# Token scatter by quarters with one semaphore each, first expert tiles from pair one, last batch regrouped in six and four tiles

## The chip, the cores and the metric

The program runs on one core of one Trainium2 chip. The metric is device time in microseconds. Five engines work side by side and meet through semaphores: TensorE (PE, with PEld for its weight loads), VectorE (DVE), ScalarE (ACT), GpSimd (POOL) and SyncE (SP), which issues most DMAs.

## The reference

The input is 8 batches of 512 tokens with 128 features. Each token is normalised; then two branches are added to the input:

```
xn = layernorm(x)
x  = x + mamba(xn) + moe(xn)
mamba: project to 2*256 channels, causal convolution and silu in both directions,
       dA = exp(delta*A), dBx = delta*B*u, h[l] = dA[l]*h[l-1] + dBx[l]  (16 states per channel),
       y = sum over states of h*C + D*u, times silu(z), both directions added, projected to 128
moe:   16 experts, 4 chosen per token by score; softmax gates over the four;
       expert e: w2[e] @ gelu(w1[e] @ xn + b1[e]) + b2[e]; gated sum of the four
```

## The kernel before, in words

The program has three stages.

**Preparation.** For each of the 8 batches PE, ACT and DVE compute the scan's inputs and store them in DRAM. DVE does for each batch a convolution (L1382, then twelve chained L1387), L1404, and pairs of L1409, L1415, L1422 and L1428. In the same time POOL scatters the tokens to their experts: each token's row (128 features, an id, a gate) goes to four slots of `slots_d`. There are four rounds k, one for each chosen expert. A round copies the gates of all 32 token tiles into the rows `xn` (L758, one copy of 128x32), waits for the copy, and issues 32 indirect DMAs (L762), one for each tile of 128 tokens. As the next round overwrites the gates in the rows, it first waits until all 32 DMAs of the last round have landed. All of them count on the semaphore `scattered`. SP waits for the whole count in `read_first` before it reads the first two expert tiles.

**Scan.** Eight batches follow, each in 32 steps called pairs. A pair q has two states (j = 0, 1) of 128 channels: ACT makes the decays (L1001), PE puts the B rows in PSUM (L1231, L1234), DVE multiplies where needed (L1478) and scans (two L1490), POOL multiplies the states by C (L794), PE adds them up (L1170). In some pairs DVE does the product instead (L1498): pairs 1, 4 and 7 of the first batch (`FIRST_VECTOR`) and the last ten pairs of the last batch (`LAST_VECTOR`). A state lives in a ring of 8, so DVE can be at most 8 pairs ahead of the sums.

Beside the pairs, PE and ACT compute the 80 expert tiles of 256 slots, ten in each batch. A written order (`EVENTS`, `FIRST`, `LAST`) says at which pair PE does each event: T turns the rows of a tile (L1184), U0 and U1 are the two halves of the first layer (L1191), D is the second layer (L1199), G and O are the Mamba output projection of the batch before, X and Y prepare the next batch. PE is in order: an event at pair q stands behind the B rows of pair q and ahead of those of pair q+1. ACT empties the event's PSUM bank two to four pairs later, and runs gelu for a group of tiles in one go (L969). After a D, ACT scales the rows (L947) and POOL adds them with an indirect DMA into one of two accumulators in DRAM (L779), by even and odd tile. In the first batch T comes at pairs 5, 7, 9, 11, 13, then as in the others.

**Tail.** SP reads the stored Mamba outputs (`mixed_d`) and both accumulators (L704). DVE adds them (L1537, L1543, L1545, L1548), and SP stores the result.

Of the kernel before, what the change touches and what calls it, by code (L numbers as in the profile page):

```python
# [14 lines left out]
D = 128  # L15
BATCH, L = 8, 512
TOK = BATCH * L
NT = TOK // P
TPB = L // P
DIN = 256  # L20
NH = DIN // P
# [5 lines left out]
E, TOPK = 16, 4  # L27
FF = 512
FC = FF // P
# [4 lines left out]
MPB = NTILE // BATCH  # L34
# [24 lines left out]

FIRST_VECTOR = (1, 4, 7)  # L60
VECTOR = ()
# [79 lines left out]

FIRST_T = [5, 7, 9, 11, 13] + T_STEP[GROUP:]
FIRST_U = [q + 2 for q in FIRST_T]
# [3 lines left out]
for _j in range(MPB):  # L147
    FIRST[FIRST_T[_j]].append(("T", _j, 1, False))
    if _j >= GROUP:
        FIRST[FIRST_T[_j] + 1].append(("D", _j - GROUP, 0, False))  # L150


LAST_T = [0, 2, 4, 7, 9, 12, 15, 17, 20, 22]
LAST_U = [2, 4, 6, 9, 11, 13, 16, 18, 21, 23]
LAST_D = [(1, 5, True), (3, 6, True), (5, 7, True), (8, 8, True), (10, 9, True), (17, 0, False), (19, 1, False),
          (22, 2, False), (24, 3, False), (25, 4, False), (27, 5, False), (28, 6, False), (29, 7, False), (30, 8, False),
          (31, 9, False)]
LAST = [[] for _ in range(PAIRS)]
# [8 lines left out]
LAST_LAG = 4  # L167
LAST_GELU = [16, 28]
LAST_BURSTS = [[12, 13], [24, 25]]
LAST_STEP = [p + (LAST_LAG - 2 if p < 6 or 15 < p < 19 else LAST_LAG - 1 if p < 9 or 13 < p < 22 or p == 26 else  # L170
# [47 lines left out]
def hidden_slot(b, j):  # L218

    if isinstance(b, int) and b == BATCH - 1 and j >= GROUP:  # L220
        return j if j < GROUP + 2 else j - GROUP - 2
    return j % GROUP
# [15 lines left out]
WTS_DMAS = 7  # L238
XQ = 4
XN_ACT = 3  # L240
DEST_LAG = 1
# [16 lines left out]
def wait(eng, semaphore, value):  # L258

    if not isinstance(value, int) or value > 0:  # L260
        eng.wait_ge(semaphore, value)
# [13 lines left out]
def bank_written(eng, sems, b, what, j, m, before=False):  # L275

    wait(eng, sems[f"m{m}_ready"], uses(b, m, what, j, before) + 1)
# [7 lines left out]
def bank_emptied(eng, sems, b, what, j, m, before=False):  # L285

    wait(eng, sems[f"m{m}_free"], uses(b, m, what, j, before) + 1)


def build_kernel(nc, x_in, consts_in, chan_in, inw_in, xproj_in, dtw_in, outw_in,  # L290
                 route_in, b2_in, w1_in, w2_in, out):
    with ExitStack() as ctx:  # L292
# [3 lines left out]
        def sem(name):  # L296
            return ctx.enter_context(nc.semaphore(name))
# [59 lines left out]
        def carve(n):  # L357
# [13 lines left out]
        state = carve(H_RING * 2 * L).rearrange("p (r j l) -> p r j l", r=H_RING, j=2)  # L371
        late = delta[:, 0].rearrange("p q l -> p (q l)").rearrange("p (t f s) -> p t f s", t=2, f=FC)
        hidden_all = carve(GROUP * FC * S)
        hidden = hidden_all.rearrange("p (t f s) -> p t f s", t=GROUP, f=FC)
        hidden = [hidden[:, t] for t in range(GROUP)] + [late[:, t] for t in range(2)]

        acc = [t[:, 0:BATCH * TPB * D].rearrange("p (b n) -> p b n", b=BATCH)
               for t in (decay.rearrange("p r j l -> p (r j l)"), hidden_all)]
        scanned = [t[:, 0, :, :].rearrange("p q l -> p (q l)").rearrange("p (b n) -> p b n", b=BATCH // 2) for t in (delta, du)]
# [80 lines left out]
            kw_ready bias_ready behind_ready experts_ready xn_act_ready shift_ready score_ps score_ready sel_ready logit_ps keys_ps chosen_ready rank_ps pos_ready gdiff_ready gexp_ready  # L460
            gates_ready tag_ready ids_ready acc_filled scattered v_chain pad_ready drop_ready xz_ps
            xpad_ready z_ps z_sb v_ready u_ready xd_ps xd_sb part1_ready
# [5 lines left out]
            mixed_out mixed_in sp_step pool_step acc_ready acc_last out_done"""  # L468
        s = {n: sem(n) for n in names.split()}
        x_loaded = [sem(f"x_in{i}") for i in range(XQ)]  # L470
        c_in = [sem(f"c_in{i}") for i in range(C_RING)]
# [24 lines left out]
        def _(sp):  # L496
# [78 lines left out]
            def read_first():  # L575

                sp.wait_ge(s["scattered"], 16 * NT * TOPK)
                sp.wait_ge(s["b2_out"], 16)
                sp.wait_ge(s["experts_ready"], 1)
                for j in range(W_RING):  # L580
                    read_up(j, j, j)
                    read_down(j, j)
# [70 lines left out]
            def batch(b, par):  # L653
                last = isinstance(b, int) and b == BATCH - 1
                for q in range(PAIRS + 2):
# [24 lines left out]
                    if 1 <= q <= PAIRS:  # L680
                        reload(b, q - 1)

            for r in range(C_RING):
# [8 lines left out]

            sp.wait_ge(s["mixed_out"], 16 * (BATCH - 1))
            for j in (GROUP, GROUP + 1):
                m = [e[2] for step in LAST for e in step if e[:2] == ("D", j) and not e[3]][0]
                bank_written(sp, s, BATCH - 1, "D", j, m)
            half = BATCH // 2
            for k, n in ((0, half), (1, half - 1)):
                sp.dma_start(scanned[k][:, 0:n, :], mixed_d[k * half:k * half + n].rearrange("b p n -> p b n")).then_inc(s["mixed_in"], 16)
            sp.wait_ge(s["scan_done"], DECAYS * BATCH)  # L700
            for i in range(W_RING):
# [23 lines left out]
        def _(pool):  # L725
# [28 lines left out]
            pool.wait_ge(s["gates_ready"], 1)  # L754
            for k in range(TOPK):

                wait(pool, s["scattered"], 16 * NT * k)
                nc.gpsimd.tensor_copy(xn[:, :, D + 1], gates[:, :, k]).then_inc(s["tag_ready"], 1)  # L758
                pool.wait_ge(s["tag_ready"], k + 1)
                pool.wait_ge(s["pos_ready"], min(k, 1) + 1)  # L760
                for t in range(NT):
                    pool.indirect_dma_start(slots_d, bass.IndirectOffsetOnAxis(  # L762
                        ap=pos[:, t * TOPK + k:t * TOPK + k + 1], axis=0), xn[:, t, :], None).then_inc(s["scattered"], 16)
            pool.wait_ge(s["acc_filled"], 16 * ACC_DMAS)
# [46 lines left out]
        def _(act):  # L811
# [119 lines left out]
            def empty(b, q, par=None):  # L931

                for what, j, m, before in events(b, q):
                    bank = m_ps[m]
                    bank_written(act, s, b, what, j, m, before)
                    if what == "T":
                        last = nc.scalar.copy(rowsT[:, :], bank[:, 0:S])
                    elif what in ("U0", "U1"):
                        for f in range(2):
                            c = 2 * (what == "U1") + f  # L940
                            last = nc.scalar.activation(hidden[hidden_slot(b, j)][:, c, :], bank[:, f * S:(f + 1) * S], ACT.Identity,  # L941
                                                        bias=w1[:, j % W_RING, FF + c:FF + c + 1])
# [17 lines left out]
            def gelus(b, n, now, bursts):  # L960

                for k in range(GROUP):
                    if not isinstance(b, int) or 0 <= b < BATCH:
                        if k == 0:

                            for what, m in (("U0", 1), ("U1", 0)):
                                bank_emptied(act, s, b, what, GROUP * (n + 1) - 1, m)
                        h = hidden[hidden_slot(b, GROUP * n + k)].rearrange("p f s -> p (f s)")
                        nc.scalar.activation(h, h, ACT.Gelu).then_inc(s["gelu_done"], 1)  # L969
                    if k in (1, 3):  # L970
                        empty(now, bursts[k // 2])
# [286 lines left out]
        def _(dve):  # L1258
# [274 lines left out]

            dve.wait_ge(s["mixed_in"], 32)
            for b in range(BATCH - 1):
# [75 lines left out]
```

## Time and profile before

| | us |
|---|---|
| median of 3 runs (1123.13 to 1128.26) | 1124.62 |
| the profiled execution's own time | 1122.8 |
| its span, first to last instruction | 1121.0 |
| DVE busy | 1035.2 (92%) |
| ACT busy | 938.8 (84%) |
| PE busy | 928.8 (83%) |
| POOL busy | 910.8 (81%) |
| mean granted TensorE clock | 0.943 |

The busy shares are means over the three stages. Preparation runs to about 253 us, the scan to about 1097 us, the tail to the end. An engine's row in a timeline gives its start, its duration and, in brackets, how long the engine was idle before it and what ended that idle time.

### The profile page before, as it was taken

What the parts mean: (1) busy time and instruction counts of PE and PEld (TensorE: products, weight loads), DVE (VectorE), ACT (ScalarE), POOL (GpSimd) and SP (SyncE); (2) the same over time, 40 slices, a digit from 0 to 9 for tenths busy, and PEclk for the clock granted to TensorE, in tenths of its full rate; (3) what the DMA queues carried; (4) which work ended last, traced back from release to release, by engine and by line L of the source; (5) the groups of instructions that cost most, each with busy time, mean ns of one, the idle gap of its engine ahead of it and who ended that gap; (6) DMA issues with size and microseconds to landing.
All of it is one profiled execution on the core that took longest, in us unless ns stands there. A gap on an engine that the chain in (4) does not pass through costs nothing. (4 is left out here: it accounts for less than half of the span.)

```text
span 1121.0 us, 21799 instructions
## 1 busy us (share of the span) xinstructions
PE 928.8 (83%) x5866; PEld 737.1 (66%) x5866; DVE 1035.2 (92%) x1356; ACT 938.8 (84%) x1732; POOL 910.8 (81%) x552
## 2 busy tenths in 40 slices
PE   5476887663889999999999989899999999987993
PEld 2233332232778787878887877788788777877872
DVE  8878998859999999999999989999999999986996
ACT  5258888865899999999999989999899999987940
POOL 4277878657579999999999998989999999986771
PEclk9789989775899999999999999999999999998996
DMA  9974565486756877687677767777876877665568
GB/s 304 365 253 185 193 228 191 164 295 208 238 163 175 219 192 208 182 235 194 188 207 208 194 174 212 198 196 180 233 201 162 233 192 206 164 164 142 126 143 250
DMA packets 153027, 228.87 MB, mean 204 GB/s; under 512 B 36220, under 2 KB 97948, under 8 KB 147620
## 3 DMA queue, kind: packets, MB, share of 16 engines
q1 hardware_dynamic: 125764, 208.39, 58.7%
q0 software_dynamic: 27136, 19.02, 11.8%
q8 instruction: 51, 0.84, 0.3%
q14 instruction: 76, 0.62, 0.2%
HBM read 161.84 MB, written 69.64 MB: 207 GB/s over the span
## 5 line engine op out<-in xcount | busy, mean ns | idle before, releaser
L1490 DVE TENSOR_TENSOR_SCAN arena<-arena,ps 128x512 f32<-128x512 f32 x512 | 598.1, 1202 | 0.6
L794 POOL TENSOR_TENSOR arena<-arena 128x1024 f32<-128x1024 f32 x243 | 521.1, 2476 | 49.8 <-DVE arena L1490 49.6
L1001 ACT ACTIVATE arena<-delta,a_neg 128x511 f32<-128x511 f32 x512 | 340.9, 728 | 6.7 <-DVE arena L1437 3.3
L779 POOL DMA_INDIRECT acc_d<-yrows,tags x160 | 253.3, 1583 | 46.5 <-issue 37.1
L1170 PE MATMUL ps<-ident,arena 128*128 128x128 f32 x2048 | 274.6, 278 | 7.5 <-POOL arena L794 5.1
L1478 DVE TENSOR_TENSOR ps<-du,ps 128x512 f32<-128x512 f32 x352 | 232.9, 677 | 27.2 <-PE ps L1234 25.1
L1170 PEld LDWEIGHTS ps<-ident,arena 128*128 128x128 f32 x2048 | 237.1, 144 | 20.6 <-POOL arena L794 5.6
L762 POOL DMA_INDIRECT slots_d<-arena,pos x128 | 152.8, 1193 | 46.3 <-issue 44.7
L1199 PE MATMUL ps<-w,arena 128*128 128x128 f32 x1248 | 173.8, 282 | 3.9 <-ACT arena L969 2.9
L1199 PEld LDWEIGHTS ps<-w,arena 128*128 128x128 f32 x1248 | 153.7, 191 | 14.4 <-issue 4.9
L1191 PE MATMUL ps<-rowsT,w 128*128 128x256 f32 x640 | 153.9, 384 | 10.5 <-ACT arena L952 7.5
L922 ACT ACTIVATE arena<-arena 128x256 f32<-128x256 f32 x320 | 145.5, 511 | 0.0
L1191 PEld LDWEIGHTS ps<-rowsT,w 128*128 128x128 f32 x640 | 118.2, 192 | 29.6 <-ACT arena L952 9.3
L941 ACT ACTIVATE arena<-ps,w 128x256 f32<-128x256 f32 x312 | 123.7, 477 | 4.8 <-PE ps L1191 4.4
L1231 PE MATMUL ps<-ident,arena 128*128 128x128 f32 x640 | 95.4, 279 | 22.0 <-DVE arena L1490 17.7
L1231 PEld LDWEIGHTS ps<-ident,arena 128*128 128x128 f32 x640 | 74.7, 144 | 27.5 <-DVE arena L1490 20.0
L947 ACT ACTIVATE yrows<-ps,tags 128x128 f32<-128x128 f32 x160 | 49.8, 365 | 51.3 <-PE ps L1201 40.8
L969 ACT ACTIVATE arena<-arena 128x1024 f32<-128x1024 f32 x78 | 79.1, 1054 | 0.2
L1234 PE MATMUL ps<-parts,sel 128*128 128x512 bf16 x176 | 60.3, 396 | 12.8 <-DVE arena L1490 12.6
L1387 DVE SCALAR_TENSOR_TENSOR arena<-arena,chan 128x512 f32<-128x512 f32 x96 | 64.2, 741 | 0.0
L1184 PE MATMUL ps<-ident,rows 128*128 128x128 f32 x160 | 34.1, 296 | 33.4 <-ACT arena L941 20.6
L1084 PE MATMUL ps<-arena 128*128 128x256 f32 x64 | 24.0, 541 | 33.5 <-ACT arena L843 33.5
(150 smaller groups left out, 904.6 us busy)
## 6 DMA issues: line engine op xcount, KB each, us to landing
arena<-c_d SPq DMA_DIRECT2D x128, 512.0 KB, 4.3
w<-w_dram SPq DMA_DIRECT2D x80, 258.0 KB
w<-w_dram SPq DMA_DIRECT2D x80, 256.0 KB
rows<-slots_d SPq DMA_DIRECT2D x80, 130.0 KB
slots_d<-delta SPq DMA_DIRECT2D x5, 2015.0 KB, 19.5
delta_d<-arena SPq DMA_DIRECT2D x8, 1024.0 KB, 3.9
du_d<-delta SPq DMA_DIRECT2D x8, 1024.0 KB, 6.4
delta<-delta_d SPq DMA_DIRECT2D x8, 1024.0 KB, 7.1
```

What stands on the lines that cost most here:

```text
L762: pool.indirect_dma_start(slots_d, bass.IndirectOffsetOnAxis(ap=pos[:, t * TOPK + k:t * TOPK + k + 1], axis=0), xn[:, t, :], None).then_in ...
L779: pool.indirect_dma_start(acc_d[j % W_RING], bass.IndirectOffsetOnAxis(ap=tags[:, j, a, 0:1].bitcast(I32), axis=0), yrows[:, j % W_RING, a ...
L794: nc.gpsimd.tensor_tensor(state[:, q % H_RING], state[:, q % H_RING], c_rows[:, r % C_RING], ALU.mult).then_inc(s["prod_done"], 1)
L922: last = nc.scalar.activation(scaled_du[scaled_slot(g, j)][:, t, :], duT[:, par, t, :], ACT.Identity, scale=bT[:, par, t, n:n + 1])
L941: last = nc.scalar.activation(hidden[hidden_slot(b, j)][:, c, :], bank[:, f * S:(f + 1) * S], ACT.Identity, bias=w1[:, j % W_RING, FF + c: ...
L1001: nc.scalar.activation(decay[:, q % DA_RING, j, lo:lo + L - 1], delta[:, par, dh, lo:lo + L - 1], ACT.Exp, scale=a_neg[:, dh, 2 * g + j:2 ...
L1170: last = nc.tensor.matmul(y_ps[:, h, t * P:(t + 1) * P], state[:, q % H_RING, j, t * P:(t + 1) * P], ident[:, :], is_transpose=True, start ...
L1191: last = nc.tensor.matmul(bank[:, f * S:(f + 1) * S], w1[:, slot, c * P:(c + 1) * P], rowsT[:, :], start=True, stop=True)
L1199: nc.tensor.matmul(bank[:, a * P:(a + 1) * P], kept[:, c, a * P:(a + 1) * P], w2[:, slot, c, :], start=c == 0, stop=False)
L1231: last = nc.tensor.transpose(bank[:, t * P:(t + 1) * P], scaled_du[scaled_slot(g, j)][:, t, h * P:(h + 1) * P], ident[:, :])
L1478: nc.vector.tensor_tensor(b_ps[:, ROW[q, j], j, :], du[:, par, q % DH, :], b_row, ALU.mult)\
L1490: nc.vector.tensor_tensor_scan(state[:, q % H_RING, j, way], decay[:, q % DA_RING, j, way], b_ps[:, ROW[q, j], j, way], 0.0, ALU.mult, ALU ...
```

## The change

Three things change together.

1. The scatter. `TQ = 4` quarters of 8 token tiles each have a semaphore `scattered[g]`. A round's gates are copied by quarters, 16 copies of 128x8 in all. The first four copies come ahead of the first DMA. From the second group of 8 DMAs on, the copy for the next round of the quarter issued before this one follows each group, and waits only for that quarter's own DMAs. SP waits for the four semaphores one after the other.
2. The first batch. T comes at pairs 1, 4, 7, 10, 13 instead of 5, 7, 9, 11, 13, and DVE does no product there.
3. The last batch and the tail. The ten tiles are run through gelu in groups of six and four, at ACT steps 17 and 28, instead of five and five at 16 and 28. Some T, U and D move; the last five D come one pair earlier. The bursts emptied within the first gelu group are those of pairs 14 and 15 (G and O) instead of 12 and 13. Two hidden tiles live in `gate` and `skip` instead of `delta`, the first accumulator's landing place is no longer the decays' memory but older input's, and SP reads the stored Mamba outputs in seven DMAs from pair 20 on instead of two near the end. SP starts to read the accumulators once the last B rows are written instead of after the last scan.

```diff
-FIRST_VECTOR = (1, 4, 7)
+FIRST_VECTOR = ()
-FIRST_T = [5, 7, 9, 11, 13] + T_STEP[GROUP:]
+FIRST_T = [1, 4, 7, 10, 13] + T_STEP[GROUP:]
-LAST_T = [0, 2, 4, 7, 9, 12, 15, 17, 20, 22]
-LAST_U = [2, 4, 6, 9, 11, 13, 16, 18, 21, 23]
-LAST_D = [(1, 5, True), (3, 6, True), (5, 7, True), (8, 8, True), (10, 9, True), (17, 0, False), (19, 1, False),
-          (22, 2, False), (24, 3, False), (25, 4, False), (27, 5, False), (28, 6, False), (29, 7, False), (30, 8, False),
-          (31, 9, False)]
+LAST_T = [0, 2, 4, 7, 9, 12, 16, 18, 20, 22]
+LAST_U = [2, 4, 6, 9, 11, 13, 18, 20, 22, 23]
+LAST_D = [(1, 5, True), (3, 6, True), (5, 7, True), (8, 8, True), (10, 9, True), (16, 0, False), (19, 1, False),
+          (21, 2, False), (24, 3, False), (25, 4, False), (26, 5, False), (27, 6, False), (28, 7, False), (29, 8, False),
+          (30, 9, False)]
...
-LAST_GELU = [16, 28]
-LAST_BURSTS = [[12, 13], [24, 25]]
+MIXED_FROM = 20
+LAST_TILES = [range(GROUP + 1), range(GROUP + 1, MPB)]
+LAST_GELU = [17, 28]
+LAST_BURSTS = [[14, 15], [24, 25]]
...
-                sp.wait_ge(s["scattered"], 16 * NT * TOPK)
+                for g in range(TQ):
+                    sp.wait_ge(scattered[g], 16 * (NT // TQ) * TOPK)
+                    sp.sem_inc(s["sp_step"], 1)
...
+                    if last and MIXED_FROM <= q < MIXED_FROM + BATCH - 1:
+                        n = q - MIXED_FROM
+                        sp.dma_start(scanned[2 * n // BATCH][:, n % (BATCH // 2), :], mixed_d[n]).then_inc(s["mixed_in"], 16)
...
-            sp.wait_ge(s["scan_done"], DECAYS * BATCH)
+            sp.wait_ge(s["b_ready"], len(FILLS) * BATCH)
...
-            for k in range(TOPK):
-
-                wait(pool, s["scattered"], 16 * NT * k)
-                nc.gpsimd.tensor_copy(xn[:, :, D + 1], gates[:, :, k]).then_inc(s["tag_ready"], 1)
-                pool.wait_ge(s["tag_ready"], k + 1)
+            part = NT // TQ
+
+            def tag(n):
+
+                k, g = n // TQ, n % TQ
+                own = slice(g * part, (g + 1) * part)
+                wait(pool, scattered[g], 16 * part * k)
+                nc.gpsimd.tensor_copy(xn[:, own, D + 1], gates[:, own, k]).then_inc(s["tag_ready"], 1)
+
+            for n in range(TQ):
+                tag(n)
+            for n in range(TOPK * TQ):
+                k, g = n // TQ, n % TQ
+                pool.wait_ge(s["tag_ready"], n + 1)
                 pool.wait_ge(s["pos_ready"], min(k, 1) + 1)
-                for t in range(NT):
+                for t in range(g * part, (g + 1) * part):
                     pool.indirect_dma_start(slots_d, bass.IndirectOffsetOnAxis(
-                        ap=pos[:, t * TOPK + k:t * TOPK + k + 1], axis=0), xn[:, t, :], None).then_inc(s["scattered"], 16)
+                        ap=pos[:, t * TOPK + k:t * TOPK + k + 1], axis=0), xn[:, t, :], None).then_inc(scattered[g], 16)
+                if n > 0 and n - 1 + TQ < TOPK * TQ:
+                    tag(n - 1 + TQ)
...
-            dve.wait_ge(s["mixed_in"], 32)
+            dve.wait_ge(s["mixed_in"], 16 * (BATCH - 1))
```

## Rows read from the trace of the kernel before

**Rows 1.** The page's first part: busy time and share of each engine.
```profile
PE 928.8 (83%) x5866; PEld 737.1 (66%) x5866; DVE 1035.2 (92%) x1356; ACT 938.8 (84%) x1732; POOL 910.8 (81%) x552
```

**Rows 2.** Timeline of POOL: start, duration, line, operation; in brackets idle before it.
```profile
47.80 0.36 POOL L758 COPY arena<-gates 128x32 f32<-128x32 f32 x1 [21.72 <-DMA slots_d<-delta]
...
93.16 1.70 POOL L762 DMA_INDIRECT slots_d<-arena,pos  x1 [0.30 <-issue]
99.09 7.10 POOL L758 COPY arena<-gates 128x32 f32<-128x32 f32 x1 [4.22 <-DMA slots_d<-arena,pos]
106.46 0.98 POOL L762 DMA_INDIRECT slots_d<-arena,pos  x1 [0.28 <-POOL arena L758]
...
117.32 1.04 POOL L762 DMA_INDIRECT slots_d<-arena,pos  x1 [0.30 <-issue]
...
142.17 1.38 POOL L762 DMA_INDIRECT slots_d<-arena,pos  x1 [0.31 <-issue]
143.86 1.02 POOL L762 DMA_INDIRECT slots_d<-arena,pos  x1 [0.30 <-issue]
...
158.33 0.24 POOL L758 COPY arena<-gates 128x32 f32<-128x32 f32 x1 [1.45 <-DMA slots_d<-arena,pos]
...
207.44 0.96 POOL L762 DMA_INDIRECT slots_d<-arena,pos  x1 [0.30 <-issue]
213.19 3.93 POOL L758 COPY arena<-gates 128x32 f32<-128x32 f32 x1 [4.79 <-DMA slots_d<-arena,pos]
217.40 0.98 POOL L762 DMA_INDIRECT slots_d<-arena,pos  x1 [0.28 <-POOL arena L758]
...
240.46 0.96 POOL L762 DMA_INDIRECT slots_d<-arena,pos  x1 [0.30 <-issue]
248.63 0.97 POOL L762 DMA_INDIRECT slots_d<-arena,pos  x1 [7.22 <-issue]
...
267.99 0.96 POOL L762 DMA_INDIRECT slots_d<-arena,pos  x1 [0.30 <-issue]
```

**Rows 3.** Timeline of DVE in preparation, and at the start of the first batch.
```profile
46.30 1.75 DVE L1353 TENSOR_TENSOR arena<-arena 128x1536 f32<-128x1536 bf16 x1
...
96.92 8.03 DVE L1387 SCALAR_TENSOR_TENSOR arena<-arena,chan 128x512 f32<-128x512 f32 x12
104.87 1.22 DVE L1404 TENSOR_SCALAR du<-arena 128x2048 f32<-128x2048 f32 x1
...
119.06 8.03 DVE L1387 SCALAR_TENSOR_TENSOR arena<-arena,chan 128x512 f32<-128x512 f32 x12
127.02 1.21 DVE L1404 TENSOR_SCALAR du<-arena 128x2048 f32<-128x2048 f32 x1
...
157.10 2.35 DVE L1422 SCALAR_TENSOR_TENSOR arena<-ps,arena 128x1024 f32<-128x1024 f32 x2
...
215.80 1.21 DVE L1404 TENSOR_SCALAR du<-arena 128x2048 f32<-128x2048 f32 x1
...
235.57 1.23 DVE L1404 TENSOR_SCALAR du<-arena 128x2048 f32<-128x2048 f32 x1 [7.23 <-ACT arena L874]
...
258.76 0.67 DVE L1478 TENSOR_TENSOR ps<-du,ps 128x512 f32<-128x512 f32 x1
260.58 1.23 DVE L1498 TENSOR_TENSOR arena<-arena 128x1024 f32<-128x1024 f32 x1 [1.15 <-DMA arena<-c_d]
...
271.38 4.59 DVE L1498 TENSOR_TENSOR arena<-arena 128x1024 f32<-128x1024 f32 x1
...
285.74 1.22 DVE L1498 TENSOR_TENSOR arena<-arena 128x1024 f32<-128x1024 f32 x1
```

**Rows 4.** Timeline of PE: the first T of the first batch.
```profile
275.44 0.69 PE L1184 MATMUL ps<-ident,rows 128*128 128x128 f32 x2 [1.58 <-DMA tags<-slots_d]
```

**Rows 5.** DVE's waits from 990 us on: sum, times, longest.
```profile
DVE ps L1478 <- PE ps L1234: 12.7, 5, 5.0
```

**Rows 6.** The chain of work that ended last, in order of time.
```profile
1098.48 6.76 DMA acc_d<-yrows,tags
...
1115.33 0.69 DVE arena L1548
```

More of the change, by code:

```diff
@@ L239 @@
 XQ = 4
+TQ = 4
 XN_ACT = 3
@@ L371, in build_kernel @@
         state = carve(H_RING * 2 * L).rearrange("p (r j l) -> p r j l", r=H_RING, j=2)
-        late = delta[:, 0].rearrange("p q l -> p (q l)").rearrange("p (t f s) -> p t f s", t=2, f=FC)
+        late = [flat.rearrange("p (f s) -> p f s", f=FC) for flat in (gate[:, 0].rearrange("p h t c -> p (h t c)"),
+                                                                       skip[:, 0].rearrange("p h l -> p (h l)"))]
         hidden_all = carve(GROUP * FC * S)
         hidden = hidden_all.rearrange("p (t f s) -> p t f s", t=GROUP, f=FC)
-        hidden = [hidden[:, t] for t in range(GROUP)] + [late[:, t] for t in range(2)]
+        hidden = [hidden[:, t] for t in range(GROUP)] + late
         acc = [t[:, 0:BATCH * TPB * D].rearrange("p (b n) -> p b n", b=BATCH)
-               for t in (decay.rearrange("p r j l -> p (r j l)"), hidden_all)]
+               for t in (arena[:, TURNED_AT:turned_end], hidden_all)]
         scanned = [t[:, 0, :, :].rearrange("p q l -> p (q l)").rearrange("p (b n) -> p b n", b=BATCH // 2) for t in (delta, du)]
@@ L460, in build_kernel @@
             kw_ready bias_ready behind_ready experts_ready xn_act_ready shift_ready score_ps score_ready sel_ready logit_ps keys_ps chosen_ready rank_ps pos_ready gdiff_ready gexp_ready
-            gates_ready tag_ready ids_ready acc_filled scattered v_chain pad_ready drop_ready xz_ps
+            gates_ready tag_ready ids_ready acc_filled v_chain pad_ready drop_ready xz_ps
             xpad_ready z_ps z_sb v_ready u_ready xd_ps xd_sb part1_ready
@@ L469, in build_kernel @@
         s = {n: sem(n) for n in names.split()}
+        scattered = [sem(f"scattered{i}") for i in range(TQ)]
         x_loaded = [sem(f"x_in{i}") for i in range(XQ)]
@@ L681, in batch @@
                         reload(b, q - 1)
+                    if last and q == MIXED_FROM:
+                        sp.wait_ge(s["mixed_out"], 16 * b)
+                        sp.sem_inc(s["sp_step"], 1)
+                        sp.wait_ge(s["decay_ready"], DECAYS * b)
+                        sp.sem_inc(s["sp_step"], 1)
+                        sp.wait_ge(s["dbx_done"], len(DBX) * b)
+                        sp.sem_inc(s["sp_step"], 1)
+                    if last and MIXED_FROM <= q < MIXED_FROM + BATCH - 1:
+                        n = q - MIXED_FROM
+                        sp.dma_start(scanned[2 * n // BATCH][:, n % (BATCH // 2), :], mixed_d[n]).then_inc(s["mixed_in"], 16)
             for r in range(C_RING):
@@ L691, in _ @@
             batch(BATCH - 1, 1)
[L693 to L699, printed above, removed]
-            sp.wait_ge(s["scan_done"], DECAYS * BATCH)
+            sp.wait_ge(s["b_ready"], len(FILLS) * BATCH)
             for i in range(W_RING):
@@ L938, in empty @@
                     elif what in ("U0", "U1"):
+                        if isinstance(b, int) and b == BATCH - 1 and j == GROUP:
+                            act.wait_ge(s["y_free"], NH * b)
                         for f in range(2):
@@ L960, in gelus @@
             def gelus(b, n, now, bursts):
-                for k in range(GROUP):
+                tiles = LAST_TILES[n] if isinstance(b, int) and b == BATCH - 1 else range(GROUP * n, GROUP * (n + 1))
+                for k, j in enumerate(tiles):
                     if not isinstance(b, int) or 0 <= b < BATCH:
@@ L966, in gelus @@
                             for what, m in (("U0", 1), ("U1", 0)):
-                                bank_emptied(act, s, b, what, GROUP * (n + 1) - 1, m)
-                        h = hidden[hidden_slot(b, GROUP * n + k)].rearrange("p f s -> p (f s)")
+                                bank_emptied(act, s, b, what, tiles[-1], m)
+                        h = hidden[hidden_slot(b, j)].rearrange("p f s -> p (f s)")
                         nc.scalar.activation(h, h, ACT.Gelu).then_inc(s["gelu_done"], 1)
```

## The prediction

> **What bounds the kernel now.** I read the page's busy shares first. DVE is busy for 92% of the span and no other engine for more than 84% [rows 1], so in the scan a microsecond that DVE stands still is a microsecond of time. I then read POOL's and DVE's timelines beside each other, because the change rewrites POOL's scatter and the question is what it meets. The reader is to see two things. First, the scatter ends late: its last DMA is issued at 267.99 and ends at 268.95 [rows 2], while DVE is already at the third pair of the first batch at 258.76 [rows 3]. It costs little today, since the first T stands at pair 5: PE turns the first rows at 275.44 [rows 4], 6.5 us after the scatter's end, and DVE uses the eight decays made ahead and has its own products meanwhile. Second, the gate copies L758 take 0.36, 7.10, 0.24 and 3.93 us for the same 128x32 elements [rows 2]. The last views are DVE's waits in the last batch and the chain that ends last: five waits for B rows, 12.7 us [rows 5], and then an accumulating DMA that lands at 1105.24, and adds up to 1116.0 [rows 6].
>
> **Why the copies differ.** I set the end of each beside DVE's work. The copy of 99.09 ends at 106.19; DVE's L1387 run and the L1404 behind it end at 106.09. The copy of 213.19 ends at 217.12; L1404 ends at 217.01. The copy of 47.80 ends at 48.16; L1353 ends at 48.05. The copy of 158.33 takes 0.24 and lies in L1422, which reads one input from PSUM [rows 2, 3]. So three copies end 0.1 us after a stretch in which DVE reads two inputs from SBUF or runs L1404, and the fourth, in another kind of work, does not wait. The 7.10 us cover about nine starts of L1387 (8.03 us for twelve, 0.66 apart), and the copy came in at none of them.
>
> The Trainium skill (SBUF — State Buffer, "Who interferes with whom") says that VectorE and GpSimd lock a shared port pair for one whole instruction, whoever is first. By that rule a copy would wait at most for one DVE instruction; the 7.10 us speak for a whole run. What the rule alone would give is the first rival below.
>
> **Part 1, the scatter: what it removes.** Between rounds POOL stands from 94.86 to 106.46 and from 208.40 to 217.40, and about 2.2 us around the copy of 158.33 (1.45 idle, 0.24, and the step to the next DMA, 0.48) [rows 2]. That is 22.8 us, of which 0.9 us stay as three ordinary gaps of 0.3. The landing waits in it (4.22, 1.45, 4.79) do go: a copy now waits for DMAs issued a whole group earlier.
>
> **What it adds.** There are 16 copies instead of 4; three more at the start and twelve between groups. Unhindered each costs 0.24 and a step of 0.3: 12 x 0.54 = 6.5, and 0.7 for the three. But behind a waiting copy stand the next eight DMAs, as POOL is in order, and the twelve fall where they fall in DVE's pattern. That pattern repeats every 22.15 us (L1404 at 104.87 and 127.02), and its blocked stretch before the end of L1404 begins at the latest with L1387 at 119.06, 8 us and more before 127.02. Eight DMAs take 11.9 us (106.46 to 118.36) [rows 2, 3]. So a group that starts at the end of an L1404 finishes 12 us later; the copy behind it arrives at 118.7, when DVE is just before or in its L1387 run, and is let through at 128.3. The next group starts there, and the same happens again: POOL is held to one group of eight per 22.15 us where it now does nearly two.
>
> I walk it through. Groups 0 and 1 start as now. The copies behind groups 1, 2 and 3 meet earlier stretches; I take 3.6 us each, half of the 7.1 seen, and get to the L1404 end at 106.1 with four groups issued, where the kernel before has the same 32 DMAs out. Groups 4 to 8 end with copies let through at 128.2, 150.4, 172.5, 194.7 and 217.0 (the last is the L1404 of 215.80). At 217.0 the changed kernel has issued nine groups, 72 DMAs; before it was 96, and the last 32 took 51.6 us from 217.40, with a gap of 7.2 ahead of 248.63 in it [rows 2]. From there DVE's blocked stretches are few (it idles 7.2 us before 235.57 [rows 3], and the scan reads only one input from SBUF per instruction). The seven groups left cost 51.6 for four, three more at 10.3, and 2.2 for the four copies left: 84.7. The scatter ends at about 302 instead of 269. If the 7.2 us gap does not recur it is 295; if a copy at 241 meets DVE's next stretch it is 306.
>
> **Part 2, first tiles from pair one.** SP's reads and PE's first T followed the end of the scatter by 6.5 us [rows 2, 4], so T comes at 308.5. It now stands at pair 1, ahead of the B rows of pair 2. DVE therefore stops where it stood at 258.76 [rows 3] and goes on about 1.5 us after T, at 310.0: 51.2 us lost. ACT waits for the same T at its step 3, with decays 0 to 3 made, which it catches up in the 3.3 us that a pair takes. The three DVE products go: 1.15 idle and 1.1 at 260.58, 4.5 at 271.38 (it waited for POOL), 1.1 at 285.74, together 7.9 us [rows 3]. POOL takes them over; it starts its products only at 302, but DVE has just two pairs done then, so POOL is not late. PE starts cold after 50 us of idleness and T moves closer to U: I add 1. The first batch: +51.2 - 7.9 + 1 = +44.
>
> **Part 3, last batch and tail.** DVE's 12.7 us of waits [rows 5] lie around the gelu group, where G and O wait for ACT. They are now emptied within the group, but the T and U that moved and a group of six take some of it: bounds 0 and -12.7, or up to +13 if the new order stalls PE as often again; I take -3.5. The last D come one pair earlier, 3.3 to 3.5 us; the final landing at 1105.24 and the adds behind it [rows 6] move with them: -3.5 (bounds 0 and -6). The earlier reads of the first accumulator and of `mixed_d` lie beside the scan and count nothing by themselves. Together -7.
>
> **Sum.** +44 - 7 = +37 on the profiled execution's 1122.8 gives 1159.8, say 1160. The median of the runs is 1.8 above that execution, which is within their spread.
>
> **The rivals.**
> *The copy slips in between two DVE instructions* (the other side: faster). For it speaks that the scatter's own DMAs get through the L1387 run with 1.38 and 1.02 us [rows 2], so something of POOL's enters at DVE's instruction boundaries, and a copy of 8 columns may need less than one of 32; the skill's rule of one instruction says the same. Against it are the nine boundaries that a copy missed. The scatter then ends at 268.95 - 22.8 + 0.9 + 6.5 + 0.7 = 254.3, or 259 with 0.4 us of waiting per copy. T comes at 261 to 266, DVE loses 3.5 to 8.5, saves 7.9, and the last batch gives 7: 1111 to 1116, say 1114. It turns slower once the scatter ends later than about 266.
> *The copy waits for some boundaries, fewer than 32 columns did.* Half way between 254 and 302 the scatter ends at 278; DVE goes on at 286.2, +27.4 - 7.9 - 7 + 1 = +13.5: 1136. The same evidence speaks for and against it.
>
> **How the numbers follow.** Held by whole runs, 1160: 0.52, its own range 1152 to 1168. Slipping in, 1114: 0.33. Between, 1136: 0.15. The range goes from 1112 to 1166, which leaves out the lower part of the second case and the last of the first. This kernel's runs can tell about 0.5% (5.6 us) from no change. Of the slipping case 0.30 is faster; 0.03 of it and 0.02 of the middle case fall within 0.5%; slower is 0.65.
>
> **What would show it.** In the changed kernel's timeline of POOL: copies L758-like of 4 to 10 us that end 0.1 us after an L1404, five of them 22.15 us apart between 128 and 217; last scatter DMA near 302; DVE idle for some 50 us from 259, ended by PE's B rows; PE's first T near 308. In the last batch, waits for B rows of 9 us instead of 12.7. The prediction is wrong if the copies take 0.2 to 1 us and the scatter ends before 262.

## The result, and the profile after

The changed kernel takes 1120.16 us, the median of 15 runs (1107.52 to 1123.82), beside 1126.61 (15 runs, 1115.77 to 1137.39) of the kernel before: a ratio of 0.9946 [0.9921, 0.9972]. It is faster by a little more than the 0.5% that can be told from no change. The prediction, 1160 and slower, was wrong, though its range of 1112 to 1166 holds the time; its first rival gave 1114. The profiled execution took 1119.97, with a span of 1118.1. The page of the kernel after answers to [rows 1]:

```profile
PE 936.8 (84%) x5866; PEld 740.8 (66%) x5866; DVE 1025.5 (92%) x1353; ACT 938.3 (84%) x1732; POOL 913.3 (82%) x567
```

POOL's timeline after (start, us, engine, line, operation, out<-in, shape, count, and in brackets the idle time before it with what ended it) answers to [rows 2]. L773 is the old L758, L782 the old L762.

```profile
47.34 1.25 POOL L773 COPY arena<-gates 128x8 f32<-128x8 f32 x4 [21.77 <-DMA slots_d<-delta]
...
108.68 0.21 POOL L773 COPY arena<-gates 128x8 f32<-128x8 f32 x1
...
121.39 0.24 POOL L773 COPY arena<-gates 128x8 f32<-128x8 f32 x1
...
134.13 0.35 POOL L773 COPY arena<-gates 128x8 f32<-128x8 f32 x1
...
146.55 0.54 POOL L773 COPY arena<-gates 128x8 f32<-128x8 f32 x1
...
171.75 0.55 POOL L773 COPY arena<-gates 128x8 f32<-128x8 f32 x1
...
210.44 0.20 POOL L773 COPY arena<-gates 128x8 f32<-128x8 f32 x1
...
244.39 1.74 POOL L782 DMA_INDIRECT slots_d<-arena,pos  x1 [0.31 <-issue]
...
267.55 3.95 POOL L816 TENSOR_TENSOR arena<-arena 128x1024 f32<-128x1024 f32 x2 [21.42 <-DVE arena L1515]
```

DVE's timeline after answers to [rows 3]; L1412 is the old L1387, the long run in which a copy was held, and L1503 the first work of the scan (old L1478).

```profile
120.83 8.03 DVE L1412 SCALAR_TENSOR_TENSOR arena<-arena,chan 128x512 f32<-128x512 f32 x12
...
142.98 8.04 DVE L1412 SCALAR_TENSOR_TENSOR arena<-arena,chan 128x512 f32<-128x512 f32 x12
...
166.86 8.03 DVE L1412 SCALAR_TENSOR_TENSOR arena<-arena,chan 128x512 f32<-128x512 f32 x12
...
261.70 0.70 DVE L1503 TENSOR_TENSOR ps<-du,ps 128x512 f32<-128x512 f32 x1 [2.03 <-issue]
...
276.16 1.29 DVE L1503 TENSOR_TENSOR ps<-du,ps 128x512 f32<-128x512 f32 x2 [8.71 <-PE ps L1259]
```

The twelve copies between groups, of which six stand here, take 0.20 to 0.56 us each. Of the six, three arrive inside an L1412 run (121.39, 146.55, 171.75). The scatter ends at 246.1, 22.8 us before the 268.95 of [rows 2], and POOL then has nothing to do for 21.4 us. Yet DVE waits 8.71 us for PE's first B rows. The reason stands in SP's queue, before and after, and in PE's timeline (answers to [rows 4]):

```profile
258.12 0.33 SPq L533 DMA_DIRECT2D parts<-parts_d  x1
271.30 0.36 SPq L552 DMA_DIRECT2D w<-w_dram  x1
271.71 0.43 SPq L553 DMA_DIRECT2D rows<-slots_d  x1
```
```profile
259.64 0.33 SPq L595 DMA_DIRECT2D du_d<-delta  x1
263.79 1.76 SPq L633 DMA_DIRECT2D arena<-c_d  x4
267.76 0.36 SPq L557 DMA_DIRECT2D w<-w_dram  x1
268.17 0.57 SPq L558 DMA_DIRECT2D rows<-slots_d  x1
```
```profile
275.01 0.69 PE L1209 MATMUL ps<-ident,rows 128*128 128x128 f32 x2 [15.28 <-DMA tags<-slots_d]
```

In the kernel before, SP was through with its other work at 258.45 and issued nothing until 271.30, after the scatter's end. In the changed kernel the scatter has long ended. The scattered rows are read from 268.17, behind the stores of the prepared data and the C rows, and PE turns them at 275.01: as late as the 275.44 of before, with the scatter 22.8 us earlier. Preparation itself is 8.6 us longer in this execution; by SP's two queues the T would come at about 267 without that (an estimate: 258.45, the 1.82 us from there to the rows' read after, and 6.84 to the T).

DVE's waits from 990 us on (answers to [rows 5]: us in total, times, longest) and the chain that ended last (answers to [rows 6]):

```profile
DVE ps L1503 <- PE ps L1259: 7.9, 6, 2.2
DVE gated L1489 <- PE ps L1195: 1.5, 1, 1.5
```
```profile
1096.76 5.92 DMA acc_d<-yrows,tags
1105.43 5.60 DMA arena<-acc_d
```

I cut both executions at four marks of DVE: the first work of the scan, and the first multiplication by the gate (old L1464) for the first batch, for the last but one, and for the last.

```
                 before  after   difference
scan starts      253.10  261.70  +8.6
first batch      118.6   116.7   -1.9
middle           607.3   606.4   -0.9
last batch       118.9   115.0   -3.9
tail, to the end  23.1    18.4   -4.8
span            1121.0  1118.1   -2.9
```

### The profile page after: what moved, and what is told of

Read it like the earlier page. It is cut to its first block, busy times and chain, and to the rows that moved or that the text cites. A ratio compares the mean times of both kernels' runs of the same rounds, so it can differ in the third digit from the quotient of the medians.

```text
span 1118.1 us, 21844 instructions
## 1 busy us (share of the span) xinstructions
PE 936.8 (84%) x5866; PEld 740.8 (66%) x5866; DVE 1025.5 (92%) x1353; ACT 938.3 (84%) x1732; POOL 913.3 (82%) x567
## 4 chain that ended last, share of the span: by engine, by line
issue 22%; POOL 22%; ACT 17%; PE 10%; DMA 3%; DVE 2%; POOLq 0%; SPq 0%; ACTq 0%; DVEq 0%
POOL arena L816 13%; POOL acc_d L801 9%; ACT arena L1026 6%; PE ps L1224 3%; ACT arena L965 2%; ACT arena L944 2%; PE ps L1195 2%; ACT arena L994 2%; PE ps L1256 1%; PE ps L1216 1%; ACT yrows L971 1%; DMA acc_d<-yrows,tags 1%; DVE arena L1515 1%; ACT L1026 1%; ACT L994 1%
## 5 line engine op out<-in xcount | busy, mean ns | idle before, releaser
L816 POOL TENSOR_TENSOR arena<-arena 128x1024 f32<-128x1024 f32 x246 | 527.2, 2469 | 66.7 <-DVE arena L1515 66.6
L1195 PE MATMUL ps<-ident,arena 128*128 128x128 f32 x2048 | 270.7, 276 | 3.5 <-DVE arena L1523 3.5
L1503 DVE TENSOR_TENSOR ps<-du,ps 128x512 f32<-128x512 f32 x352 | 233.1, 678 | 27.9 <-PE ps L1259 25.8
L1195 PEld LDWEIGHTS ps<-ident,arena 128*128 128x128 f32 x2048 | 233.1, 142 | 15.5 <-DVE arena L1523 4.0
L782 POOL DMA_INDIRECT slots_d<-arena,pos x128 | 156.1, 1219 | 37.1 <-issue 35.0
L1256 PE MATMUL ps<-ident,arena 128*128 128x128 f32 x640 | 95.1, 278 | 18.8 <-DVE arena L1515 14.5
L1256 PEld LDWEIGHTS ps<-ident,arena 128*128 128x128 f32 x640 | 74.4, 143 | 24.7 <-DVE arena L1515 16.6
L1412 DVE SCALAR_TENSOR_TENSOR arena<-arena,chan 128x512 f32<-128x512 f32 x96 | 64.2, 741 | 0.0
L1209 PEld LDWEIGHTS ps<-ident,rows 128*128 128x128 f32 x160 | 18.4, 142 | 62.4 <-ACT arena L965 21.6
```

The lines of the kernel that those rows point to most:

```text
L782: pool.indirect_dma_start(slots_d, bass.IndirectOffsetOnAxis(ap=pos[:, t * TOPK + k:t * TOPK + k + 1], axis=0), xn[:, t, :], None).then_in ...
L816: nc.gpsimd.tensor_tensor(state[:, q % H_RING], state[:, q % H_RING], c_rows[:, r % C_RING], ALU.mult).then_inc(s["prod_done"], 1)
L1195: last = nc.tensor.matmul(y_ps[:, h, t * P:(t + 1) * P], state[:, q % H_RING, j, t * P:(t + 1) * P], ident[:, :], is_transpose=True, start ...
L1256: last = nc.tensor.transpose(bank[:, t * P:(t + 1) * P], scaled_du[scaled_slot(g, j)][:, t, h * P:(h + 1) * P], ident[:, :])
L1503: nc.vector.tensor_tensor(b_ps[:, ROW[q, j], j, :], du[:, par, q % DH, :], b_row, ALU.mult)\
```

## The experiments

Ratios are to runs of the kernel before on the same chip, with 95% intervals; without one there was a single execution. The expectations speak of two theories. Theory A: the scatter is off the path, the gain is all in the last batch and the tail, and the longer preparation is chance. Theory B: POOL's new rhythm lengthens preparation. In the edits, "..." stands for lines left out.

### The parts one by one

**s1_scatter**: the kernel before with the scatter by quarters alone.
```diff
...
-                wait(pool, s["scattered"], 16 * NT * k)
-                nc.gpsimd.tensor_copy(xn[:, :, D + 1], gates[:, :, k]).then_inc(s["tag_ready"], 1)
...
+                wait(pool, scattered[g], 16 * part * k)
+                nc.gpsimd.tensor_copy(xn[:, own, D + 1], gates[:, own, k]).then_inc(s["tag_ready"], 1)
...
```


> The kernel before with the scatter by quarters alone. Theory A: the scatter ends at about 246 instead of 269, and nearly nothing follows: 0 to 3 us faster (the DVE product that waited 3.4 us for POOL). Theory B: 6 to 9 us slower, with the first scan product at 261. What the prediction held (copies stopped by DVE's runs): the scatter ends at 302, with copies of 4 to 10 us.

Measured: 1128.81, ratio 0.9988 [0.9945, 1.0031]. The scatter ends at 245.6, the scan starts at 263.26, and no time that could be told from noise comes of it.

**s12_scatter_first**: the same, and the first tiles from pair one.
```diff
-FIRST_VECTOR = (1, 4, 7)
+FIRST_VECTOR = ()
-FIRST_T = [5, 7, 9, 11, 13] + T_STEP[GROUP:]
+FIRST_T = [1, 4, 7, 10, 13] + T_STEP[GROUP:]
...
```


> The kernel before with the scatter by quarters and the first batch's new order (T from pair one, no DVE product), without the last batch's part. Theory A: DVE waits about 9 us for the first tile's rows and saves 3.4 us of products, so 4 to 6 us slower than the scatter alone, that is 1 to 6 us slower than the kernel before. If the first two parts were what makes the changed kernel faster, 4 to 8 us faster.

Measured: 1132.39, ratio 1.0035 [0.9996, 1.0075]. DVE waits 8.7 us for the first rows, and the first batch takes 116.9 beside 113.0 in s1_scatter.

**s3_last**: the kernel before with the last batch and tail of the change alone (`LAST_*`, `LAST_TILES`, the reads of `mixed_d` from pair 20, the accumulator in another buffer).
```diff
...
-LAST_GELU = [16, 28]
-LAST_BURSTS = [[12, 13], [24, 25]]
+LAST_TILES = [range(GROUP + 1), range(GROUP + 1, MPB)]
+LAST_GELU = [17, 28]
+LAST_BURSTS = [[14, 15], [24, 25]]
...
```


> The kernel before with the last batch regrouped and the tail's reads moved, alone. Theory A: 8 to 9 us faster (3.9 between the last two gate products, 4.8 in the tail, as in the changed kernel's trace). Rival: the tail's share depends on the earlier end of something in the first parts, then 4 us or less.

Measured: 1116.11, ratio 0.9908 [0.9877, 0.9939]. The last batch takes 110.3 (118.9 before), the tail 18.4 (23.1). This part alone gives as much as the whole change or more.

**a_again**: the changed kernel itself, timed beside these.

> The changed kernel once more, beside the others on one chip. Theory A (the scatter is off the path, the gain is all in the last batch and the tail; the first batch loses as much to the wait for the first rows as it wins by the three products; the longer preparation in the profiled execution was TensorE's clock by chance): 6 us under the kernel before, scan start anywhere between 252 and 262. Theory B (POOL's new rhythm itself lengthens the preparation): the first scan product starts at 261 again, 8 us later than the kernel before does.

Measured: 1119.21, ratio 0.9921 [0.9889, 0.9953]. The scan starts at 264.12, not by 262 as Theory A had it, and DVE's wait is there again:
```profile
279.32 1.29 DVE L1503 TENSOR_TENSOR ps<-du,ps 128x512 f32<-128x512 f32 x2 [9.45 <-PE ps L1259]
```

### What holds a copy

**c_split_copy**: the kernel before, each round's copy cut into four of 8 columns, all behind the same wait for the landing.
```diff
-                nc.gpsimd.tensor_copy(xn[:, :, D + 1], gates[:, :, k]).then_inc(s["tag_ready"], 1)
-                pool.wait_ge(s["tag_ready"], k + 1)
+                for g in range(4):
+                    own = slice(g * NT // 4, (g + 1) * NT // 4)
+                    nc.gpsimd.tensor_copy(xn[:, own, D + 1], gates[:, own, k]).then_inc(s["tag_ready"], 1)
+                pool.wait_ge(s["tag_ready"], 4 * k + 4)
```


> The kernel before with each round's gate copy cut into four copies of 128x8, issued one behind the other after the same landing wait. If a copy is held in a run of L1387 because it has 32 columns, those that fall into such a run take 0.2 to 0.6 us each, none over 1.2. If it is held because it arrives after an idle stretch of POOL (a landing wait), the first of the four takes up to 7 us where it falls into a run.

Measured: 1122.25. Timelines of POOL and DVE:
```profile
98.89 7.19 POOL L760 COPY arena<-gates 128x8 f32<-128x8 f32 x1 [4.09 <-DMA slots_d<-arena,pos]
...
214.12 3.37 POOL L760 COPY arena<-gates 128x8 f32<-128x8 f32 x4 [2.70 <-DMA slots_d<-arena,pos]
```
```profile
96.85 8.03 DVE L1389 SCALAR_TENSOR_TENSOR arena<-arena,chan 128x512 f32<-128x512 f32 x12
104.81 1.21 DVE L1406 TENSOR_SCALAR du<-arena 128x2048 f32<-128x2048 f32 x1
```
A copy of 8 columns is held for 7.19 us, and is through 0.06 us after DVE's L1406 (end 106.02). So a copy need not be wide to be held. The first copy of another round meets DVE's two instructions of 128x1024 at 159.25 instead, and takes 1.12 us, to just behind the end of the first of them.

**c_wide_copy**: the changed kernel with a copy of 32 columns behind each of 8, and POOL not idle before it.
```diff
...
                 nc.gpsimd.tensor_copy(xn[:, own, D + 1], gates[:, own, k]).then_inc(s["tag_ready"], 1)
+                wait(pool, s["wide_done"], n)
+                nc.gpsimd.tensor_copy(wide[:, :, 0], gates[:, :, k]).then_inc(s["wide_done"], 1)
```


> The changed kernel with a second copy, of all 32 columns of gates into a scratch tile with two words per column, behind each copy of 8; POOL is never idle before it. If the size decides, those that fall into a run of twelve chained DVE instructions take several us and end 0.1 us after the L1404-like instruction behind the run, about five of them, and the scatter ends near 290. If the arrival after idleness decides, or the wide stride of the destination (130 words), all stay under 1.3 us and the scatter ends near 255.

Measured: 1121.04. POOL, and DVE's run beside it:
```profile
121.61 0.96 POOL L785 DMA_INDIRECT slots_d<-arena,pos  x1 [0.30 <-issue]
122.57 0.24 POOL L774 COPY arena<-gates 128x8 f32<-128x8 f32 x1
122.76 0.75 POOL L776 COPY wide<-gates 128x32 f32<-128x32 f32 x1
```
```profile
122.02 8.03 DVE L1415 SCALAR_TENSOR_TENSOR arena<-arena,chan 128x512 f32<-128x512 f32 x12
```
All the wide copies take 0.22 to 1.26 us, this one inside a run of the kind that held a copy of 8 columns in c_split_copy.

**c_idle**: the changed kernel, where POOL waits for the landing of the group just issued ahead of each of the twelve copies between groups. The copies keep their width and order.
```diff
                 if n > 0 and n - 1 + TQ < TOPK * TQ:
+                    pool.wait_ge(scattered[g], 16 * part * (k + 1))
                     tag(n - 1 + TQ)
```


> The changed kernel, where POOL waits for the landing of the group just issued ahead of each of the twelve gate copies, so that each copy of 128x8 comes after 3 to 6 us of idleness. If arrival after idleness is what lets DVE's run of twelve hold a copy, those that fall into such a run take up to 9 us and end 0.1 us after the L1404-like instruction, three or more of them; the scatter then ends near or beyond 300. If the phase is all, they stay under 1.3 us and the scatter ends near 300 by the landing waits alone (twelve of 4 to 5 us).

Measured: 1166.96. POOL and DVE:
```profile
125.14 5.77 POOL L773 COPY arena<-gates 128x8 f32<-128x8 f32 x1 [5.51 <-DMA slots_d<-arena,pos]
147.83 6.86 POOL L773 COPY arena<-gates 128x8 f32<-128x8 f32 x1 [4.41 <-DMA slots_d<-arena,pos]
171.07 7.42 POOL L773 COPY arena<-gates 128x8 f32<-128x8 f32 x1 [3.86 <-DMA slots_d<-arena,pos]
...
196.87 5.47 POOL L773 COPY arena<-gates 128x8 f32<-128x8 f32 x1 [5.81 <-DMA slots_d<-arena,pos]
```
```profile
121.68 8.04 DVE L1413 SCALAR_TENSOR_TENSOR arena<-arena,chan 128x512 f32<-128x512 f32 x12
129.63 1.22 DVE L1430 TENSOR_SCALAR du<-arena 128x2048 f32<-128x2048 f32 x1
...
169.26 8.03 DVE L1413 SCALAR_TENSOR_TENSOR arena<-arena,chan 128x512 f32<-128x512 f32 x12
177.21 1.21 DVE L1430 TENSOR_SCALAR du<-arena 128x2048 f32<-128x2048 f32 x1
...
325.23 1.29 DVE L1504 TENSOR_TENSOR ps<-du,ps 128x512 f32<-128x512 f32 x2 [55.47 <-PE ps L1260]
```
Six of the twelve copies arrive between 104 and 220, all inside an L1413 run. They take 2.70 to 7.42 us, and each ends some 0.06 us after the L1430 behind it: 125.14 + 5.77 = 130.91, and 129.63 + 1.22 = 130.85. Of the other six, idle before too but outside such a run, four take 0.20, one 0.32 beside DVE's 128x1024 instructions of 1.2 us, and one 1.00, to 0.06 us after a DVE instruction of 1.48. The scatter ends at 317.95, and DVE stands 55.47 us. The twelve added waits are 47.4 us in all and are in this time too.

**c_memset**: the kernel before with a memset of 128x32, which reads nothing, between the landing wait and the copy.
```diff
...
+                nc.gpsimd.memset(idle[:, k, :], 0.0)
                 nc.gpsimd.tensor_copy(xn[:, :, D + 1], gates[:, :, k]).then_inc(s["tag_ready"], 1)
```


> The kernel before with a small memset of 128x32 (it reads nothing) behind the landing wait, ahead of each gate copy. If only the first instruction after idleness is held, whatever it does, the memset takes the time and the copy is short, or nothing is held at all because a memset needs no read; if it is the first instruction that reads SBUF, the copy is held for 3 to 8 us as before where it falls into a run.

Measured: 1122.98.
```profile
99.51 0.12 POOL L759 MEMSET idle<- 128x32 f32 x1 [4.22 <-DMA slots_d<-arena,pos]
99.58 7.03 POOL L760 COPY arena<-gates 128x32 f32<-128x32 f32 x1
```
The memset is not held, and the copy right behind it is. It isn't enough that some instruction of POOL ran just before.

### The wait for the first rows

**e_early_reads**: the changed kernel with both tiles' reads on SP directly behind the last store of `parts`.
```diff
                 store(b, parts_d, parts_p.rearrange("p d l -> p (d l)"), "parts_ready", "parts_out")
+                if b == BATCH - 1:
+                    read_first()
...
-                        if isinstance(b, int) and b == 0:
-                            read_first()
```


> The changed kernel with SP's reads of the first two expert tiles moved ahead, behind the store of the last batch's parts, instead of behind the signal that all preparation is done. If DVE's 8.7 us wait in the first batch is the place of the reads in SP's queue, as Theory A says, the wait is under 1 us and the kernel is 8 us faster than the changed one, about 14 under the kernel before. If it is the landing of the scatter or DMA traffic, the wait stays at 5 to 9 us and the time with it.

Measured: 1112.16, ratio 0.9878 [0.9843, 0.9914]. The wait for rows is gone and the first batch takes 108.1, but the reads hold SP from 255.10 to 262.08, `delta` is stored after them, and DVE stands 5.54 us ahead of the scan instead of 2.03.

**e_split_reads**: tile 0 is read behind the last store of `parts`, tile 1 behind the last of `du`.
```diff
...
+                if b == BATCH - 1:
+                    read_first()
...
             store_prepared(BATCH - 1)
+            read_up(1, 1, 1)
+            read_down(1, 1)
...
```


> The changed kernel with the reads of tile 0 behind the store of the last parts and those of tile 1 behind the last store of all, so that the seven microseconds of issuing no longer hold back the store of delta. In the run with both tiles ahead the scan began 3.5 us late (5.54 us idle instead of 2.03). If SP's queue is the cause, the idle time is back at 2.0 and the wait for the first rows stays under 1 us: 3 us faster than that run, some 17 under the kernel before, and faster than all kernels so far.

Measured: 1109.31, ratio 0.9862 [0.9820, 0.9904]. First batch 109.3. The time is as expected, the start of the scan is not: 4.50 us of idle time ahead of it are left, where 2.0 were expected.

**g_reads_behind_stores**: `read_first()` behind all stores of the last batch, ahead of SP's wait for `prepared`.
```diff
             store_prepared(BATCH - 1)
+            read_first()
             sp.wait_ge(s["prepared"], 1)
...
-                        if isinstance(b, int) and b == 0:
-                            read_first()
```


> The changed kernel with SP's reads of the first two tiles behind the last store of the preparation, ahead of the wait for all preparation. With the reads ahead of the store of delta the scan began 2.5 to 3.5 us late. If that store is what the scan's start waits for, the idle time before the first scan product is 2.0 again and the first rows come within 2 us of DVE's need: 1106 to 1110, at least as fast as the split reads. If the DMA traffic of the reads themselves delays the start, nothing is won over the 1109.3 of that kernel.

Measured: 1112.75, ratio 0.9899 [0.9858, 0.9940]. The scan starts after its usual 2.01, and there is no wait for the first rows, but one of 3.12 for B rows later. First batch 111.3. The expected 1106 to 1110 was missed.

**f_late_tiles**: the changed kernel with the first tiles back at pair five, and DVE's three products still gone.
```diff
-FIRST_T = [1, 4, 7, 10, 13] + T_STEP[GROUP:]
+FIRST_T = [5, 7, 9, 11, 13] + T_STEP[GROUP:]
```


> The changed kernel with T back at pairs 5, 7, 9, 11, 13 and still no DVE product. Theory A: the 9 us wait of DVE for the first rows goes (under 1 us), and with it 5 to 9 us of time, 1111 to 1115. If the products were needed because POOL or PE is late with few tiles placed early, the gain is under 3 us.

Measured: 1110.29, ratio 0.9864 [0.9810, 0.9918]. No wait for the first rows, first batch 109.4. Putting this one list back takes 9 us off the changed kernel, by the two ratios (0.9946 - 0.9864) x 1127; by the changed kernel's repeat, a_again, it is 6, and in the traces the first batch is 7.3 shorter.

All four are clear of the kernel before, and below the changed kernel in the middle value. The intervals of e_early_reads, e_split_reads and f_late_tiles lie below that of the changed kernel, 0.9921 to 0.9972; that of g_reads_behind_stores overlaps with it, and all four overlap with that of its repeat (0.9889 to 0.9953). The four aren't told apart from each other.

## Why the prediction was wrong

**The step that failed** is the one that put the copies into DVE's pattern: the copy "arrives at 118.7, when DVE is just before or in its L1387 run, and is let through at 128.3". The copies did arrive there, and weren't held: 0.24 at 121.39, 0.54 at 146.55. The hold that I read in [rows 2, 3] is real and has two conditions, of which I had only one. It needs DVE's run of L1387, and it needs that the copy stands behind a landing wait. The four copies of [rows 2] all do, so the rows could not show the second; the change lets its twelve copies come without such a wait. c_idle puts such a wait ahead of each and changes nothing else: six of the six copies that meet the run are held, for up to 7.42 us. Its rhythm is the one that I walked, one group of eight for each of DVE's batches. That its end is near mine (scatter 302 predicted and 317.95 measured, DVE's stop 51.2 and 55.47, time 1160 and 1166.96) is in part luck, as 47.4 us of added waits are in it, which the walk did not have. c_split_copy and c_wide_copy exclude the width.

The clue was in [rows 2]: DMAs on the same engine get through the L1387 run with 1.38 and 1.02. I gave it to the rival and did not ask how they differ from the copy: each follows the one before by 0.30, and the held copies stand 4.22 and 4.79 us after the last DMA. The Trainium skill (SBUF — State Buffer, "Who interferes with whom") has the port pair locked for one whole instruction. The 0.24 to 0.56 us of the back-to-back copies agree with that, an L1412 instruction being 0.66; the 2.7 to 7.4 of c_idle do not.

Why a copy gets in when POOL has just issued a DMA, or has just copied, is not settled. A memset just before doesn't help it, so either memset takes no part in what decides, or it is the DMA that opens the way. Nor is it settled that POOL's idleness decides: wherever a copy was held, the scatter DMAs issued before it had landed, and wherever one got in within such a run, POOL had just issued another. No run separates these. The kernel before shows something like it once with the engines the other way round: POOL has three products back to back, and DVE's product of 271.38 in [rows 3], which follows another DVE instruction without a gap, ends at 275.97, 1.10 us after the last of them (274.87):

```profile
268.97 5.90 POOL L794 TENSOR_TENSOR arena<-arena 128x1024 f32<-128x1024 f32 x3
```

The boundary between POOL's second and third product lies at about 272.9, and DVE's product did not come in there.

**Rival 1** had the copies and the scatter nearly right (254 to 259 predicted; 246.1, because the gap of 7.2 us ahead of 248.63 did not recur, and no copy took over 0.56). But its gain from there was wrong. It set T 6.5 us behind the scatter, at 261 to 266; T came at 275.01 in the changed kernel, 28.9 us behind it. This is the second step that failed, in the prediction as in the rival. In [rows 2, 4] the 6.5 us are SP's reads and their landing, since there the scatter ended last. But two things are waited for at that place, the scatter and the end of preparation with SP's queue behind it, and I took the one that came last for the only one. s1_scatter shows what follows: 23 us off the scatter, ratio 0.9988 [0.9945, 1.0031]. That the rival's 1114 is near is luck in this: part 2 cost time where it had a gain or nearly nothing, and part 3 alone gave more than its 7.

**Part 2, the products**, at -7.9. In [rows 3] 4.59 of it was a slow product beside POOL. In s3_last they are three of 1.2, in s1_scatter one of 2.83 and two of 1.21. Against it stands the wait for the first rows, 8.7 to 9.5, that T at pair 1 exposes. Worked out for the two traces: 8.7 in s12_scatter_first less some 5.0 of products in s1_scatter gives +3.7, and their first batches are 116.9 and 113.0. By the ratios it is (1.0035 - 0.9988) x 1127 = 5.3 us, but the two intervals overlap, so that this number alone shows nothing. The +1 for PE's cold start was 0.3 in c_idle: DVE waits 46.0 us longer there than in a_again, and the first batch takes 46.3 longer (163.4 and 117.1), with a granted clock of 0.51 from 320 to 330 us and 1.00 from 330 to 340. f_late_tiles, without the wait, has the first batch at 109.4 instead of 116.7.

**Part 3**, -7, with its mechanism right and the size low: 12.7 us of waits became 7.9, the last batch -3.9 in the changed kernel's trace and -8.6 in s3_last, the tail -4.8 in both, within the bounds that I gave for it. As a ratio s3_last gives 0.9908, 10.4 us. This is the whole gain. The shares of s12_scatter_first and s3_last multiply to 1.0035 x 0.9908 = 0.9943, and 0.9946 is measured; the intervals are 0.003 to 0.004 to either side, so a fit this close is luck.

**The signs in the profile** that I named for a wrong prediction are those that came: copies of 0.2 to 1 us, and a scatter that ends before 262.

## What to carry to other kernels

A stall seen only behind a wait may belong to the wait. Before it is charged to instructions that will no longer wait, look for a neighbour on the same engine that met the same traffic without waiting. And before an early end is counted as gain, list everything that its consumer waits for, its queue included: here a scatter 23 us earlier gave a ratio of 0.9988 [0.9945, 1.0031], since SP's reads stood behind stores that hadn't moved, and a transfer pulled forward pays only if its issue is pulled forward too, in a gap of the queue (e_split_reads: 0.9862 beside 0.9946 and, in the repeat, 0.9921).

## What the runs showed of the hardware that was not expected

**The preparation differs by some 10 us between executions.** The scan starts at 253.10 in the kernel before and at 261.70 after, with the same 5866 matmuls of PE. The windows show TensorE's granted clock (columns: us, busy time and count of PE, PEld, DVE, ACT and POOL, granted clock, DMA share, GB/s), before, after, and in f_late_tiles:

```profile
128.00:176.00 48.00, 35.63 (x83) 15.27 (x82) 41.60 (x53) 41.77 (x40) 37.54 (x31) 0.93 0.52 192
176.00:223.00 47.00, 32.91 (x77) 14.44 (x77) 42.77 (x54) 40.75 (x39) 34.93 (x26) 0.88 0.51 188
```
```profile
128.00:176.00 48.00, 40.64 (x80) 17.79 (x78) 42.19 (x53) 37.84 (x37) 39.44 (x35) 0.79 0.51 187
176.00:223.00 47.00, 40.80 (x80) 18.05 (x80) 39.54 (x51) 37.39 (x37) 38.29 (x34) 0.78 0.52 191
```
```profile
128.00:176.00 48.00, 37.54 (x88) 16.03 (x87) 43.75 (x56) 41.40 (x40) 39.43 (x35) 0.93 0.52 190
176.00:223.00 47.00, 35.15 (x78) 14.95 (x76) 40.79 (x51) 38.99 (x38) 38.59 (x33) 0.88 0.53 196
```

The levels are 2.4 and 1.2 GHz; a mean of 0.78 over a stretch is some of each. Eight matmuls of the same line take, before and after:
```profile
142.38 3.60 PE L1116 MATMUL ps<-arena 128*128 128x512 f32 x8
```
```profile
168.74 6.22 PE L1141 MATMUL ps<-arena 128*128 128x512 f32 x8
```
I first thought that the new rhythm of POOL did it. f_late_tiles and e_split_reads have the new scatter and the high clock (scan at 258.8 and 260.9, the latter with 4.50 us of idle time ahead of it instead of 2.0); s3_last has the old scatter and 0.78 (scan at 267.9). So neither scatter brings either clock with certainty. Nor do the odds look different. In the fourteen traces the mean clock of the whole span is 0.940 or more where preparation had the high clock, and 0.934 or less where not. By the same mark, over the executions of the changed kernel and of every comparison with an interval, 23 of 60 with the old scatter are at 0.940 or more, and 29 of 75 with the new. The +8.6 of the first table is therefore not shown to be of the change's making, and it hides most of part 3's gain when one profile is set against one other. Executions of like clock show that gain at either level: in a_again's comparison the changed kernel takes 1112.0 and the kernel before 1122.8 in the middle at 0.940 or more, and 1121.3 and 1126.5 below it.

**A short preparation uncovers the scatter.** With the scan at 253.1 the first batch of the kernel before takes 118.6. In s3_last, with the same scatter (end 258.6) and the same first batch, the scan starts at 267.9 and it takes 111.6. Of the 7.0 us about 3.4 are the slow product of 271.38 beside POOL's late ones, 2.7 are waits for B rows and 1.1 one for C rows. Part of what the clock gives is lost again in the first batch. It also means that the early scatter, worth nothing in the mean, may be worth something where preparation is short: the three executions of s1_scatter at 0.940 or more take 1113.1 to 1118.6, and the thirteen of the kernel before beside them 1119.4 to 1129.1. Three are few, and s12_scatter_first does not repeat it (three at 1119.9 to 1122.2, five of the kernel before at 1118.9 to 1122.2); there the wait for the first rows stands against it.
